# One more half tile of the second FFN product in seven products, a last block in two halves, and no dummy products ahead of the first projection

## The reference

```python
uv = layernorm(x) @ in_proj_w + in_proj_b        # 512 -> 1024
u, v = uv[..., :D], uv[..., D:]
v_local = depthwise_conv3(silu(v)) + conv_b
y = scan(v_local)                                # h = a*h + ssm_b*v ; y = ssm_c*h + ssm_d*v, along the rows
out = (u * silu(y)) @ out_proj_w + out_proj_b
x = x + layernorm(layernorm(out + residual) * ln_w + ln_b)
h = gelu(layernorm(x) @ ternary(W1).T + b1)      # 512 -> 2048
x = x + layernorm(h @ ternary(W2).T + b2)        # 2048 -> 512
```

## Time and profile before

| | before |
|---|---|
| median of three runs (lowest, highest) | 1385.47 us (1384.61, 1386.35) |
| the profiled execution's own time | 1385.97 us |
| its span, first to last instruction | 1384.2 us |
| TensorE busy | 1364.4 us (99%) |
| VectorE busy | 1273.3 us (92%) |
| ScalarE busy | 1076.1 us (78%) |
| GpSimd busy | 396.1 us (29%) |

### The profile page before, as it was taken

How to read it: one execution, slowest core, us unless ns; L and a number is a source line. 1 busy time by engine, 2 the same in 40 slices (tenths; PEclk the granted TensorE clock), 3 DMA queues, 4 the chain that set the end, 5 groups by cost and what they waited for, 6 DMA issues and landing times.

```text
span 1384.2 us, 26015 instructions
## 1 busy us (share of the span) xinstructions
PE 1364.4 (99%) x9674; PEld 949.1 (69%) x9674; DVE 1273.3 (92%) x2236; ACT 1076.1 (78%) x1644; POOL 396.1 (29%) x548
## 2 busy tenths in 40 slices
PE   7999999999999999999999999999999999999997
PEld 4444555768777676776768767676776768765884
DVE  7999989889999999998999999999998999988984
ACT  7999585788877878777788877888778788994653
POOL 5135133132421314232141321414223141232212
PEclk9999999999999999999999999999999999999999
DMA  8732422333323334132343223334132342202212
GB/s 238 253 119 50 115 51 62 70 54 93 43 58 67 49 92 62 47 68 62 70 62 79 47 59 69 54 92 62 47 62 46 93 62 62 32 1 62 37 27 61
DMA packets 164654, 98.18 MB, mean 71 GB/s; under 512 B 133680, under 2 KB 133680, under 8 KB 164400
## 3 DMA queue, kind: packets, MB, share of 16 engines
q1 hardware_dynamic: 155888, 80.79, 23.2%
q0 software_dynamic: 8640, 15.73, 9.0%
HBM read 31.49 MB, written 32.51 MB: 46 GB/s over the span
## 4 chain that ended last, share of the span: by engine, by line
PE 90%; DVE 2%; issue 1%; ACT 0%; POOL 0%; POOLq 0%; DVEq 0%; ACTq 0%
PE f2b L703 23%; PE f1b L664 15%; PE f1b L663 15%; PE misc L627 7%; PE misc L625 7%; PE misc L626 7%; PE misc L639 4%; PE misc L640 4%; PE misc L641 4%; PE f2b L689 2%; PE f2b L687 2%; PE f2b L740 1%; PE f2b L741 1%; PE f1b L669 0%; PE f1b L670 0%
## 5 line engine op out<-in xcount | busy, mean ns | idle before, releaser
L664 PE MATMUL f1b<-x3T,w 128*128 128x256 f16 x1792 | 396.7, 273 | 0.0
L663 PE MATMUL f1b<-x3T,w 128*128 128x256 f16 x1792 | 396.7, 272 | 0.0
L2576 ACT ACTIVATE ring<-f1b,par 128x256 f32<-128x256 f32 x480 | 197.7, 469 | 95.2 <-PE f1b L664 82.3
L703 PE MATMUL f2b<-stage,ring 128*128 128x256 fp8e5 x1456 | 218.4, 273 | 0.0
L1138 DVE SCALAR_TENSOR_TENSOR ring<-ring,f_sc 128x896 f16<-128x896 f32 (+1 forms) x196 | 206.6, 1062 | 6.1 <-ACT ring L2599 3.8
L2599 ACT ACTIVATE ring<-ring,f_sc 128x1792 f16<-128x1792 f32 x104 | 185.8, 1786 | 26.3 <-DVE ring L1196 26.1
L703 PE MATMUL f2b<-w,ring 128*128 128x256 fp8e5 x1092 | 203.4, 273 | 0.1
L663 PEld LDWEIGHTS f1b<-x3T,w 128*128 128x128 fp8e5 x1792 | 175.3, 98 | 24.1
L664 PEld LDWEIGHTS f1b<-x3T,w 128*128 128x128 fp8e5 x1792 | 175.3, 98 | 24.1
L627 PE MATMUL misc<-x1T,win_lo 128*128 128x512 f16 x456 | 172.8, 379 | 0.0
L626 PE MATMUL misc<-x1T,win_hi 128*128 128x512 f16 x456 | 172.8, 379 | 0.0
(11 more groups left out here) (276 smaller groups left out, 2838.1 us busy)
## 6 DMA issues: line engine op xcount, KB each, us to landing
out_dram<-xs SPq DMA_DIRECT2D x60, 256.0 KB, 2.1
xs<-x_dram SPq DMA_DIRECT2D x14, 1024.0 KB, 5.7
out_dram<-hb POOLq DMA_DIRECT2D x32, 256.0 KB, 4.1
out_dram<-stage POOLq DMA_DIRECT2D x28, 256.0 KB, 4.1
ring<-w1t_dram SPq DMA_DIRECT2D x4, 1024.0 KB, 14.0
stage<-w2t_dram SPq DMA_DIRECT2D x3, 1024.0 KB, 7.9
x1T<-tp SPq DMA_TRANSPOSE x68, 3.2
xs<-x_dram SPq DMA_DIRECT2D x4, 256.0 KB, 4.1
```

The source lines that it names most:

```text
L663: pe.matmul(o_, w, src[:, k, h * TH:(h + 1) * TH], start=k == 0, stop=False)
L664: mm = pe.matmul(o_, w, src[:, KC + k, h * TH:(h + 1) * TH], start=False, stop=k == KC - 1)
L703: return pe.matmul(bank_[:, cols], a, b, start=start and p == 0, stop=stop and p == PAIRS - 1, skip_group_check=True)
L2576: ins = act.activation(g_of(t, j)[:, ts], f1b[i % 2][:, ts], ACT.Gelu, bias=par[:, B1 + chunk:B1 + chunk + 1], scale=1.0 / ACT_SCALE)
```

## The change

Three things are changed in what is done: `seven` also holds for tile 1, h = 1; of the last tile's block 3, each product of 512 columns is two of 256, the right half into another PSUM bank, and the five last units of the left half are made ahead of the right half's, with `last_half`, `last_stats` and `last_aggr` on VectorE; and the 18 dummy products behind `win_sum(1)` are gone. Of the other work of the end, block 2 is now centred on ScalarE (`last_shift`) and finished with `last_out(2)`.

```diff
-        return 1 < t < NT - 3 or t == NT - 2 or t in (NT - 3, NT - 1) and h == 0
+        return 1 < t < NT - 3 or t == NT - 2 or (t, h) in ((1, 1), (NT - 3, 0), (NT - 1, 0))
...
+        last_cols, last_banks = (slice(0, TH), slice(TH, 2 * TH)), (3, 1)
...
             def f2_last():
 
-                for q in (2, 3):
+                for j in range(FC - LAG_END, FC):
+                    pe.wait_ge(hl_ok, FC * (NT - 1) + j + 1)
+                    mm = f2_block(NT - 1, j, 2)
+                mm.then_inc(f2_sum, 1)
+                for i in range(2):
                     for j in range(FC - LAG_END, FC):
-                        if q == 2:
-                            pe.wait_ge(hl_ok, FC * (NT - 1) + j + 1)
-                        mm = f2_block(NT - 1, j, q)
+                        mm = f2_half_block(j, i)
                     mm.then_inc(f2_sum, 1)
...
             pe.wait_ge(x1_hi, 1)
             warm(6)
             win_sum(1)
-            warm(6)
-            keep_warm()
             ffn_scale()
             in_proj("v", 0, 0, v_mm)
             in_proj("v", 0, 1, v_mm)
+            in_proj("v", 0, 2, v_mm)
             win_sum(0)
-            in_proj("v", 0, 2, v_mm)
             in_proj("v", 0, 3, v_mm)
...
+            def last_half(i):
+
+                j, cols = NB - 1, last_cols[i]
+                ve_.wait_ge(f2_sum, 2 + i)
+                if i == 0:
+                    ve_.wait_ge(out_st[j], 16 * (NT - 1))
+                ve_.scalar_tensor_tensor(out=hb[:, j, cols], in0=f2b[last_banks[i]][:, cols], scalar=f_inv[:, 0:1],
+                                         in1=b2_row[:, cols], op0=ALU.mult, op1=ALU.add).then_inc(f_ok, 1)
+
+            def last_stats(i):
+
+                ve_.wait_ge(f_ok, NB * NT + i)
+                if i == 0:
+                    ve_.wait_ge(mv_ok[4], NB * (NT - 1) + 3)
+                ve_.bn_stats(raw_stats(4)[:, i, :], hb[:, NB - 1, last_cols[i]]).then_inc(bn_ok[4], 1)
...
-                rstd(4, NT - 1, rs4[:, js], j == NB - 1, js)
-                if j < NB - 1:
+                if j == NB - 2:
+                    pool.wait_ge(mv_ok[4], NB * (NT - 1) + j + 1)
+                    pool.tensor_scalar(nm4[:, js], mean_var(4)[:, js, 0], -1.0, None, ALU.mult).then_inc(nmean_ok, 1)
+                rstd(4, NT - 1, rs4[:, js], j >= NB - 2, js)
+                if j < NB - 2:
```

1261 lines of the change are left out of this document (583 added, 678 removed).

## The result

The changed kernel takes 1387.1 us (median of 21 runs, 1386.0 to 1388.16), the kernel before 1385.13 us measured beside it (21 runs, 1384.36 to 1387.23). The ratio is 1.0013, 95% interval 1.0007 to 1.0019: slower by 2.0 us by the medians and 1.8 by the ratio, where 0.7 us of gain was forecast. The time lies in the forecast's range and within its bound of 0.2%, but its sign is wrong, and the interval excludes no change.

The account below looks back on a forecast made before the run. TensorE, busy 99% of the span, was taken as the bound, VectorE 5% behind. Seven products -1.6 + 1.2, front +0.4, tail -0.7 gave -0.7: 1385.3 us profiled, 1384.8 us median, range 1382.4 to 1387.6.

Parts of the forecast that it names:

- seven products, with VectorE's price: Tile 1's second half in seven products: 1.6 us of products saved, 1.2 us of it lost to VectorE's added work.
- splits earlier: Front: VectorE's part of the fourth split comes sooner, so the first projection starts earlier: -1.3 us, ends 0 and 2.
- low clock: Front: without the dummies the first projection runs 4.9 us at the low clock: +2.4 us, ends 1.4 and 4.4.
- the wait at `win_sum(0)`: Front: TensorE no longer waits there for u's maxima, one projection block later: -0.9 us.
- VectorE's side of it, and the new order until step 3: VectorE waits for u's later scale, then is full from 80 to 100 us: +0.2, ends 0 and 2; new order 0.
- the new order in step 3: Reordering in step 3, part of the new order of the other steps, costed at nothing.
- tail: After the last product: VectorE's halved work -0.55 us, GpSimd's power 0.15 us sooner: -0.7, ends -1.0 and -0.3.
- What I cost at nothing: The last block's 64 half-width products (0.06 us) and the new order of the other steps, both taken as zero.
- VectorE's price in step 3: VectorE's sums and longer splits add 8.5 us there, making TensorE wait: 1.2 us, ends 0 and 4.2.
- The rival in which VectorE becomes the bound there: Step 3: VectorE's earlier 10.7 us of idling stays as waits, the step takes 92.4 us: 1390.9 us; chance 0.10.
- The rival that the dummies do nothing: Front: removing the dummies does not affect the clock, something else raised it at 16.9 us: 1382.4 us; chance 0.05.
- What would show it: Signs: projection near 18.2 us, slow products until about 23, step 3's VectorE load and TensorE idling, last operation's start.

Follow-up runs that it names:

- e4: The changed kernel with tile 1's second half in plain units again, without its 12 sums: 1388.47 us, ratio to before 1.0025.
- e15: e10 with tile 1's second half back in the plain form, without its sums: 1385.44 us, ratio to before 1.0001.
- e13: e10 with W_in's sum over half 0 back behind the projection's second block: 1383.57 us, ratio to before 0.9987.
- e5: The changed kernel with dummies: 10 ahead of `win_sum(1)`, 6 behind it, 4 behind each of the first two transposed blocks: 1385.0 us, ratio to before 0.9998.
- e12: e10 without any dummies behind `win_sum(1)`, and six ahead of it: 1385.58 us, ratio to before 1.0003.
- e7: The changed kernel with both e5's dummies and e6's three moves on VectorE: 1385.86 us, ratio to before 1.0003.
- e6: The changed kernel, without dummies put back, with three moves in VectorE's order at places where TensorE waited: 1387.15 us, ratio to before 1.0016.
- e2: The kernel before without its 18 dummy products behind `win_sum(1)`, nothing else changed: 1386.17 us, ratio to before 1.0010.
- e8: The kernel before with the new tail alone (halved last block and new end): 1385.07 us, ratio to before 0.9998.
- e9: The changed kernel with before's order on all engines from the first instruction to step 3, its dummies too: 1384.24 us, ratio to before 0.9985.
- e1: The changed kernel with the 18 dummy products put back behind `win_sum(1)`: 1386.43 us, ratio to before 1.0010.
- e10: e9 with the change's VectorE and ScalarE order up to W_in's splits, `win_sum(0)` behind the third block, and e5's dummies: 1383.79 us, ratio to before 0.9982.
- e14: The changed kernel with e5's dummies and, behind the splits until step 3, before's order on VectorE alone: 1391.64 us (5 runs), ratio to before 1.0041.
- e11: The changed kernel with e5's dummies and W_in's sum over half 0 back behind the projection's second block: 1388.63 us, ratio to before 1.0014.

## Why the prediction was wrong

The forecast's sum was -0.7 us; the medians say +2.0. Term by term, in its own order (the middle column adds up to the +0.1 of the profiled pair):

| term | forecast | profiled execution | by medians |
|---|---|---|---|
| seven products, with VectorE's price | -1.6 + 1.2 | -1.4 | -1.4 (e4), -1.9 (e15 and e13) |
| splits earlier | -1.3 | -1.7 | |
| low clock | +2.4 | +1.3 | +2.1 (e5), +2.0 (e12 and e13), +1.3 (e7 and e6), +1.1 with the earlier start (e2) |
| the wait at `win_sum(0)` | -0.9 | -0.9 | |
| VectorE's side of it, and the new order until step 3 | +0.2 + 0 | +2.4 | +1.4, beside a wait of 1.0 in e13 (e5 and e13) |
| the new order in step 3 | 0 | +0.8 | |
| tail | -0.7 | -0.4 | -0.2 (e8) |

**The step that failed** stands under "What I cost at nothing": "The new order of the other steps: TensorE has next to no wait there to win, and I have no reason for one." There was none to win, but waits to gain. The first two windows are 1.81 + 0.99 = 2.80 us longer; 1.33 of it is the clock, 0.9 was saved at `win_sum(0)`, so 2.80 - 1.33 + 0.9 = 2.4 us are new waits: 1.1 from 80 to 87 us, 0.9 from 90 to 165, and the rest in pieces of up to 0.2. e9, in which the order ahead of step 3 and the dummies are put back and nothing else is changed, shows it from the other side: its profiled execution starts the projection 1.20 us later than the changed kernel's and reaches the last product 1.70 us earlier. With +3.2 for the order (2.4 and 0.8) in place of 0 and of VectorE's 0.2, and the sums' 1.2 down to 0.2, the forecast's sum would have been -0.7 + 3.2 - 1.0 - 0.2 = +1.3, and 1386.8 for the median. The prediction had read the window from 80 to 100 us, with VectorE busy 19.89 of 20 us and TensorE 0.76 us idle, and this was the warning: with VectorE that full, a change of order makes someone's input late. The prediction used it for one term alone, of 0.2 us with an end at 2.

**VectorE's price in step 3** was over-estimated: 0.2 us, not 1.2. The work added was right, about 8 us more for a forecast of 8.5, and the windows of e4 and e15 show that next to none of it reaches TensorE. The 4.8 us of waits were right too, since VectorE idles 4.84 us in that step. What was wrong is the load that both were added to. The forecast took VectorE's 76.0 us from step 3 of the kernel before, and the new order leaves it 74.50 there without the sums (e4): the same step of the prediction failed again, the order costed at nothing. With 74.5 its own working gives 74.5 + 8.5 + 4.8 - 2.8 = 85.0 of 85.1 us, and no wait. The rival in which VectorE becomes the bound there falls: it kept all of the 10.7 us of the earlier trace rows as waits, and 4.8 were left.

**The clock** was right in its mechanism and in the median's size. The stretch at the low level was 2.7 us in the profiled execution, 3.4 in e2 and 3.0 in e12, not the 4.9 that was read from the dummies of before. So +2.4 fits the medians (+2.0 and +2.1) better than the traces (+1.3 to about +1.7), and that is in part luck; why most launches should lose more than the traced ones is open, since a kernel has one trace. The low level itself: products 0.427 us apart, from 18.20 on, where the prediction had worked out 0.416. The Trainium skill (TensorE: Matmul & The Clock Gate, "Wait — 56ns, not 53.3ns?") gives 426.7 ns for 512 columns; the trace agrees. The rival that the dummies do nothing falls in e2, e5, e7 and e12.

**The start** came as forecast: the change's own order was right there. It is 1.71 us earlier in the profiled pair, but starts scatter between launches: 19.53, 19.21 and 19.02 in the three traces that have the front of before with its dummies (before, e8, e9), 17.53 to 18.13 in the nine that have the early splits and no dummies in the way (mean 17.92). On average that is 1.3, as forecast, and 0.4 of the 1.9 us between the profiled pair (+0.1) and the medians (+2.0). The clock, +2.1 by medians and +1.3 in the trace, is another 0.8, and the rest is open. What the prediction did not see is that dummies kept as they were would have held the earlier start back, by about 1.1 us in e1's trace: the 18, at 0.214 us for each of their two products until 17.33, end at 19.6.

**The tail** gave 0.4, not 0.7. VectorE's halves took 0.47 and 0.43 as estimated; GpSimd's power took 0.93 beside `last_out(2)`, for 0.87 before, so none of the hoped 0.15 came. The Trainium skill (SBUF — State Buffer, "SBUF: two separate sides") had spoken against it: a VectorE operation with two inputs in SBUF and a GpSimd operation that reads SBUF exclude each other. By that rule, the trace agrees: 0.57 us alone, 0.87 to 0.93 beside such an operation. No run here took that operation away from beside the power, so the rule itself was not tried. The rest of the miss is small pieces: 0.06 us in the power itself, 0.06 between the last product's start and VectorE's (0.48 for 0.42), 0.03 in `aggr` over two sets of statistics (0.21 for 0.18). The 0.48 is again a matter of order: VectorE adds block 2 at 1373.78 in the changed kernel, 2.0 us ahead of the last product, and at 1371.11 in e8, 4.1 us ahead of it. There it is free in time, the 0.48 is 0.31, and the tail gives 0.55.

**What would show it** was named in part. The start near 18.2 came (17.82), and so did no wait at `win_sum(0)`. The clock's first record was to stand at about 23 and stood at 20.54, VectorE was to be busy 84 us or more in step 3 and was 81.2, and the last operation was to start 2.7 us after TensorE's end and starts 3.1 after it (1376.02 to 1379.15). A wait of about one us came in step 3, 0.8 us, but at 201 and 208 us and not in units 8 to 15, and the larger one was for `g_lo`: about the right size from the wrong cause, and e4 was needed to tell.

**A better version.** The change's gains can be had without its losses. e13, with the order of before until step 3, the early splits, dummies that end early, seven products and the new tail, takes 1383.57 us, ratio 0.9987 to before (0.9978 to 0.9996), and e10 0.9982 (0.9973 to 0.9991): about 2 us under before and, by the ratios, 4 under the change. The 0.7 us of step 3's own order are still in them; that was not tried.

## What to carry to other kernels

Where an engine beside the bound is nearly full over a stretch (here 19.89 of 20 us), a change of order there is a term of its own: compare the order in which the bound engine asks with the order in which the other delivers, or give the term a range as wide as the waits that such a trace shows. To price an order, put a whole section back on all engines; putting back one engine's alone, or mending single waits, moved the waits or made new ones here (e14, e6). Dummy products that keep a clock up should end before the real work's data are there, or they hold it back (e1), and when they end depends on when the clock rises in that launch (e5 and e7). And a load that is added to a neighbour engine is costed against what the new order leaves it to do, not the old one.

## What the runs showed of the hardware

- The same dummies raise the clock at different times in different launches. In the kernel before the first record stands at 16.88 us, in e8, with the same front, at 16.01, and in e9, with the same order until step 3, at 11.27: there the six dummies from 11.79 pass in 1.58 us, their products 0.11 apart and not 0.214. In e5 it stands at 17.44, in e7 with the same dummies at 13.25. The prediction read from before's trace that the six dummies from 7.7 on don't raise it; in e9 and e12 (10.81) they alone had run when it rose. The Trainium skill (TensorE: Matmul & The Clock Gate, "What's actually happening") says that the number of products at the low clock differs between runs of the same kernel; the trace agrees.
- A clock that was up falls again in the middle of the work. In e11 it halved 1.4 us after TensorE had ended a pause of 2.07 us, for 3.4 us, and cost 1.7 us beside the pause. In e14 pauses of 2.75 and 2.57 us, ahead of 57.41 and 111.93, left it up. What tells the two apart, these runs don't show.
- The column of the granted clock reads 1.00 for all that lies ahead of its first record, at the low pace too. A window of the changed kernel over its slow products shows it:

```profile
17.90:20.50 2.60, 2.60 (x7) 0.91 (x7) 2.28 (x5) 2.41 (x5) 2.43 (x4) 1.00 0.94 306
```

Seven products in 2.60 us cannot be at 0.216 each. The distance of starts tells the level there, and the column only behind the first record.
- GpSimd's power on one number per row took 0.57 us with VectorE idle, 0.57 at 1376.14 in the changed kernel, where VectorE ran `last_half(1)` out of PSUM beside it, and 0.87 to 0.93 beside an operation of VectorE with two inputs in SBUF.
